# Twelve projection sums in place of sixteen: GpSimd folds four pixels, and the value products come in two pairs

## The reference, cut to what matters

```python
x = features.reshape(b, c, h, s, w, s)                 # s = 4: patches of n = 16 pixels
reduce_feats = x.mean((3, 5))...                       # patch means
unf = ...                                              # (b, hw, n, c)
q = _ln(reduce_feats, ln_q_w, ln_q_b) @ Wq.T
kv = _ln(unf, ln_kv_w, ln_kv_b) @ Wkv.T                # k, v for each of the 16 pixels
attn = softmax(einsum('bhpd,bhpnd->bhpn', q * scale, k), axis=-1)   # over the 16 pixels
aggre = einsum('bhpn,bhpnd->bhpd', attn, v)
return reduce_feats + aggre @ proj_w.T + proj_b
```

## Time and profile before

| | us |
|---|---|
| median of 3 runs | 945.28 (944.91 to 946.49) |
| profiled execution, its time | 945.04 |
| its span, first to last instruction | 943.2 |
| busy in the span: PE / DVE / ACT / POOL | 880.8 / 746.8 / 495.2 / 436.5 |
| mean granted TensorE clock | 0.987 |

### The profile page before, as it was taken

One profiled execution on the slowest core, in us unless ns is written; L12 is line 12 of the kernel. 1 busy time (PEld: TensorE's weight loads), 2 busy tenths in 40 slices (PEclk: granted clock), 3 DMA queues, 4 the chain that ended last, 5 costly groups with the idle time before them and its releaser, 6 DMA issues.

```text
span 943.2 us, 24254 instructions
## 1 busy us (share of the span) xinstructions
PE 880.8 (93%) x9608; PEld 376.9 (40%) x9608; DVE 746.8 (79%) x1271; ACT 495.2 (52%) x767; POOL 436.5 (46%) x259
## 2 busy tenths in 40 slices
PE   5799999999999999999999999859799999999996
PEld 1234334334334334334434434323244444444443
DVE  6688788788788788788788788999577787878775
ACT  3645445445445445445445442437766665666662
POOL 3677677677667667667667661100010110101000
PEclk9999999999999999999999999979799999999999
DMA  9568878878878878878878856100000000000000
GB/s 383 138 189 241 267 208 241 261 212 239 257 219 238 254 225 234 253 230 230 247 240 227 248 154 149 32 0 1 0 1 23 13 12 23 13 23 12 23 12 35
DMA packets 49061, 141.64 MB, mean 150 GB/s; under 512 B 5440, under 2 KB 5440, under 8 KB 40768
## 3 DMA queue, kind: packets, MB, share of 16 engines
q1 hardware_dynamic: 48960, 140.17, 49.9%
HBM read 68.85 MB, written 4.19 MB: 77 GB/s over the span
## 4 chain that ended last, share of the span: by engine, by line
PE 85%; DVE 9%; issue 2%; ACT 2%; DMA 1%; POOL 0%; SPq 0%; DVEq 0%; ACTq 0%; POOLq 0%
PE ring L864 22%; PE bank_ms L836 13%; PE qp L901 12%; PE bank_sq L836 6%; PE ring L1095 5%; DVE sb_prodv L1267 4%; PE ring L1065 4%; PE bank_ms L1107 3%; PE qp L1050 2%; PE bank_sq L1095 2%; PE ring L1010 1%; PE qp L824 1%; PE bank_ms L1065 1%; PE bank_ms L1102 1%; PE ring L1086 1%
## 5 line engine op out<-in xcount | busy, mean ns | idle before, releaser
L864 PE MATMUL ring<-sb_arena,sb_wqkv 64*64 64x512 f32 x2048 | 266.6, 602 | 16.6 <-DVE sb_prodv L1267 15.1
L1267 DVE TENSOR_TENSOR sb_prodv<-ring,sb_wbc 128x1024 f32<-128x1024 f32 x128 | 154.1, 1207 | 33.0 <-PE ring L864 30.1
L1236 DVE TENSOR_TENSOR sb_prodk<-ring,sb_qbuf 128x1024 f32<-128x1024 f32 x128 | 153.3, 1219 | 18.7 <-PE ring L864 15.4
L482 POOL TENSOR_TENSOR sb_rows<-sb_arena 128x2048 f32<-128x2048 f32 x31 | 141.7, 4569 | 15.8 <-DVE sb_sum L474 15.8
L901 PEld LDWEIGHTS qp<-sb_prodv,sb_tok_w 64*64 64x64 f32 x4096 | 119.8, 133 | 52.9 <-issue 49.8
L601 POOL TENSOR_TENSOR sb_parts_q<-sb_arena,sb_const 128x512 fp32r<-128x512 f32 x15 | 15.6, 1039 | 265.8 <-DVE sb_arena L1508 265.8
L901 PE MATMUL qp<-sb_prodv,sb_tok_w 64*64 64x128 f32 x4096 | 128.5, 269 | 1.7 <-DVE sb_prodv L1267 1.7
L645 ACT ACTIVATE sb_xsq<-sb_arena 128x2048 f32<-128x2048 f32 x64 | 118.4, 1896 | 1.3 <-DMA sb_arena<-x 1.3
L864 PEld LDWEIGHTS ring<-sb_arena,sb_wqkv 64*64 64x64 f32 x2048 | 58.4, 132 | 147.9 <-issue 78.8
L566 POOL TENSOR_TENSOR sb_score<-sb_score,sb_smx 128x512 f32<-128x512 f32 x32 | 40.9, 1279 | 79.5 <-DVE sb_smx L1250 79.5
L484 POOL TENSOR_TENSOR sb_rows<-sb_rows 128x1024 f32<-128x1024 f32 x31 | 73.9, 2383 | 2.4
(11 more groups left out here) (243 smaller groups left out, 1439.7 us busy)
## 6 DMA issues: line engine op xcount, KB each, us to landing
sb_arena<-x SPq DMA_DIRECT2D x64, 1024.0 KB, 8.8
sb_wbc<-sb_wgt SPq DMA_DIRECT2D x256, 256.0 KB, 5.7
out<-sb_arena SPq DMA_DIRECT2D x16, 256.0 KB, 2.0
sb_rest_w<-rest_w SPq DMA_DIRECT2D x1, 918.5 KB, 21.4
sb_const<-const SPq DMA_DIRECT2D x1, 264.5 KB, 3.0
sb_tok_w<-tok_w SPq DMA_DIRECT2D x1, 260.5 KB, 2.9
sb_const<-const SPq DMA_DIRECT2D x1, 256.0 KB, 21.6
```

The costliest lines, as they stand in the source:

```text
L482: eng.tensor_tensor(rows[:, :, :, :], pix[:, :, 0:8], pix[:, :, 8:16], ALU.add).then_inc(sum8_ready, 1)
L864: mm = pe.matmul(ring[slot][C * half:C * half + C, i, :], image_block(w, i), x[C * i:C * i + C, m, half, c], start=True, stop=True)
L1236: dve.tensor_tensor(by_pixel(prodk[:, c]), by_pixel(ring[c % 2][:, :, :]), q[:, :, None, :].to_broadcast([P, 2, N_PIX, G32]), ALU.mult).th ...
L1267: dve.tensor_tensor(prodv[:, :, :, G32 * c:G32 * (c + 1)], by_pixel(ring[k % 2][:, :, :]), by_pixel(wbc[:, c]), ALU.mult).then_inc(values_ ...
```

## The change

- GpSimd gets a new operation, `add_pixels(u, k)`. When value product k of unit u is in `prodv`, it adds pixels 12 to 15 of that quarter's 32 patches onto pixels 8 to 11: a [128, 2, 4, 32] float32 addition in place, 256 elements in each partition. There are four in a unit.
- `project` then runs over 12 pixels, in parts 0, 1 and 2. Part 2, which reads pixels 8 to 11, waits for all four additions of its unit (`pixels_added`). Part 3 is gone.
- TensorE's order in a step becomes: keys 0, keys 1, project 0, keys 2, project 1, keys 3, project 2, scores, values 0, values 1, squares, query, values 2, values 3, means.
- GpSimd's order in a step becomes: the first halving of the patch sums of unit n+2, additions 2 and 3 of unit n-1, the other three halvings, the shift of the scores, addition 0 of unit n, the weighing, addition 1, the normalising.
- ScalarE does `query(n+2)` ahead of `pixel_mean(n+2)`. VectorE does `score_sum(n+1)` ahead of `query_var(n+2)`.

```diff
+N_PRE, N_PART = 4, 4
+N_SUM = N_PIX - N_PRE
...
+            def add_pixels(u, k):
+
+                c = VALUE_ORDER[k]
+                pool.wait_ge(values_weighted, NC * u + k + 1)
+                part = prodv[:, :, :, G32 * c:G32 * (c + 1)]
+                pool.tensor_tensor(part[:, :, N_SUM - N_PRE:N_SUM], part[:, :, N_SUM - N_PRE:N_SUM], part[:, :, N_SUM:N_PIX],
+                                   ALU.add).then_inc(pixels_added, 1)
...
             def step(n, m):
-                if not isinstance(n, int) or n + 2 < UNITS:
-                    patch_sums(pool, n + 2, (m + 2) % NF)
-                if not isinstance(n, int) or n + 1 < UNITS:
-                    softmax(n + 1)
+                if nxt2:
+                    patch_sums_first(pool, n + 2, (m + 2) % NF)
+                if prev:
+                    add_pixels(n - 1, 2)
+                    add_pixels(n - 1, 3)
+                if nxt2:
+                    patch_sums_rest(pool, n + 2)
+                if nxt:
+                    shift_scores(n + 1)
+                add_pixels(n, 0)
+                if nxt:
+                    weigh_scores(n + 1)
+                add_pixels(n, 1)
+                if nxt:
+                    norm_scores(n + 1)
             pipeline(pool, step, UNITS)
+            add_pixels(UNITS - 1, 2)
+            add_pixels(UNITS - 1, 3)
...
+                    query(n + 2, m)
                     pixel_mean(n + 2)
-                    query(n + 2, m)
...
-                for n in range(4 * part, 4 * part + 4):
+                if part == N_SUM // N_PART - 1:
+                    pe.wait_ge(pixels_added, NC * u + NC)
+                for n in range(N_PART * part, N_PART * part + N_PART):
...
-                                           prodv[rows_of, i, n, :], start=(n == 0), stop=(n == N_PIX - 1))
-                if part == 3:
+                                           prodv[rows_of, i, n, :], start=(n == 0), stop=(n == N_SUM - 1))
+                if part == N_SUM // N_PART - 1:
                     mm.then_inc(projected_mm, 1)
...
                     project(n - 1, 2)
-                    project(n - 1, 3)
                 if nxt:
                     scores(n + 1)
                 values(n, m, 0)
+                values(n, m, 1)
                 if nxt2:
                     pixel_squares(n + 2, m2)
-                values(n, m, 1)
-                if nxt2:
                     query(n + 2, m2)
...
                 values(n, m, 2)
+                values(n, m, 3)
                 if nxt2:
                     pixel_means(n + 2, m2)
-                values(n, m, 3)
...
+                if nxt:
+                    score_sum(n + 1)
                 if nxt2:
                     query_var(n + 2)
                 if nxt:
-                    score_sum(n + 1)
                     score_inverse(n + 1)
```

More of the change, by code:

```diff
@@ L242, in build @@
         values_weighted = sem("values_weighted")
+        pixels_added = sem("pixels_added")
         projected_mm = sem("projected_mm")
@@ L475, in first_patch_sums, with patch_sums_first @@
                               ALU.add).then_inc(done[3], 1)
-        def patch_sums(eng, u, m):
+        def patch_sums_first(eng, u, m):
             eng.wait_ge(x_in[m], x_count(u, m))
@@ L482, in patch_sums, with patch_sums_rest @@
             eng.tensor_tensor(rows[:, :, :, :], pix[:, :, 0:8], pix[:, :, 8:16], ALU.add).then_inc(sum8_ready, 1)
+        def patch_sums_rest(eng, u):
             eng.wait_ge(sum8_ready, u + 1)
@@ L556, in _, with scores_of, by_patch, shift_scores @@
         def _(pool):
[L557 to L563, removed]
+            def scores_of(a):
+                return a[:, :].rearrange("p (n i) -> p n i", i=G32)
+            def by_patch(a):
+                return a[:, None, :].to_broadcast([P, N_PIX, G32])
+            def shift_scores(u):
                 pool.wait_ge(score_max_ready, u + 1)
-                pool.tensor_tensor(sc, sc, spread(smx), ALU.subtract).then_inc(scores_shifted, 1)
+                pool.tensor_tensor(scores_of(score), scores_of(score), by_patch(smx), ALU.subtract).then_inc(scores_shifted, 1)
+            def weigh_scores(u):
                 pool.wait_ge(scores_exp, u + 1)
@@ L570, in softmax, with norm_scores @@
                 pool.tensor_tensor(wgt[:, :], score[:, :], rstd[:, :], ALU.mult).then_inc(weights_raw, 1)
+            def norm_scores(u):
                 pool.wait_ge(weights_raw, u + 1)
                 pool.wait_ge(inverse_sum_ready, u + 1)
-                pool.tensor_tensor(wg, wg, spread(srz), ALU.mult).then_inc(weights_ready, 1)
-            patch_sums(pool, 1, 1)
-            softmax(0)
-            def step(n, m):
-                if not isinstance(n, int) or n + 2 < UNITS:
-                    patch_sums(pool, n + 2, (m + 2) % NF)
-                if not isinstance(n, int) or n + 1 < UNITS:
-                    softmax(n + 1)
+                pool.tensor_tensor(scores_of(wgt), scores_of(wgt), by_patch(srz), ALU.mult).then_inc(weights_ready, 1)
+            def add_pixels(u, k):
[4 more added lines that the diff above has]
+                                   ALU.add).then_inc(pixels_added, 1)
+            patch_sums_first(pool, 1, 1)
+            patch_sums_rest(pool, 1)
+            shift_scores(0)
+            weigh_scores(0)
+            norm_scores(0)
+            def step(n, m):
+                prev = not isinstance(n, int) or n >= 1
+                nxt = not isinstance(n, int) or n + 1 < UNITS
+                nxt2 = not isinstance(n, int) or n + 2 < UNITS
+                if nxt2:
[13 more added lines that the diff above has]
+                    norm_scores(n + 1)
             pipeline(pool, step, UNITS)
+            add_pixels(UNITS - 1, 2)
+            add_pixels(UNITS - 1, 3)
             pool.wait_ge(rest_in, 16)
@@ L964, in last_step @@
                 values(n, m, 0)
-                for part in range(4):
+                for part in range(N_SUM // N_PART):
                     project(n - 1, part)
```

## The result

The changed kernel takes 922.37 us (median of 4 runs, 920.26 to 924.36) against 945.69 for the kernel before (4 runs). The ratio is 0.9753, 95% interval 0.9722 to 0.9784: 23 us faster, inside the range, 8 us slower than the forecast. The profiled execution took 924.28 us, its span is 922.5.

The account below looks back on a forecast made before the run. TensorE bounds: unit 17.78 us, less 0.71 stall and 0.86 projection part, plus 0.52 scores' wait, gives 16.72; 30 units and 0.2 at the end give 913.3, with 1.2 allowed for ties 914.5 us; range 909 to 926.

Parts of the forecast that it names:

- The signs of being wrong: Wrong if project 2 waits for GpSimd, an addition is above 0.82 us, or keys 2 waits for key product 0.
- A: Rival, GpSimd late: each addition costs 0.95 us instead of 0.74, or as much is lost at waits; 925 us, chance 0.13.
- B: Rival, late keys: mean square and pixel_var delay key product 0 by 0.2 to 0.4 us more; 922 us, chance 0.16.
- The stall before keys 1: On TensorE, keys 1 starts 0.71 us late, waiting for the ring slot of values 3; the new order removes this.
- The projection, and scores waiting for key product 3: On TensorE, one project part fewer saves 0.86 us; scores then stall 0.52 us, starting 2.39 us after keys 3.
- The price of an addition: On GpSimd, 0.74 us per addition, taken from the row L489 of equal size and run length; bounds 0.64 to 1.28.
- GpSimd's loop, 16.47 us with 0.25 of slack: GpSimd's loop through project 2 takes 16.47 us, 0.25 under the 16.72 us unit, so GpSimd does not decide.
- The tie at keys 2: Pixel_var on VectorE precedes key product 0, done 12.52 us after scores; TensorE reaches keys 2 at 12.56; delay lengthens the unit.
- Load of x has whole units of slack. Free.: Among the DMAs, the load of x has whole units of slack and costs nothing.
- The swaps, "costed at nothing": ScalarE's query before mean square and VectorE's sum before query_var fit in waits and cost nothing.
- The end, "net -0.2": Last unit: normalising up to 0.74 us later, projection 0.93 us shorter; net 0.2 us saved.
- the forecast's 31.8 us in the units: Gain over 30 units, each going from 17.78 to 16.72 us.

Follow-up runs that it names:

- e3: Changed kernel with only the new engine orders: 16 pixels projected in four parts, no additions; 926.65 us, unit 17.12 us.
- e4: Changed kernel with only the additions and the 12-pixel projection; value quarters and ScalarE and VectorE orders as before the change; 938.82 us, unit 17.45 us.
- e9: Changed kernel with each GpSimd addition 512 elements in place of 256; 962.25 us, unit 18.22 us.
- e6: Changed kernel with each load of x, from unit 4 on, bringing a quarter of its bytes; 918.38 us, unit 16.80 us.
- e7: Changed kernel with additions 2 and 3 ahead of the first halving on GpSimd; 917.71 us, unit 16.79 us.
- e2: Changed kernel without GpSimd's additions and without TensorE's wait for them, the projection still over 12 pixels; 916.48 us, unit 16.79 us.
- e8: Changed kernel with additions 2 and 3 ahead of the first halving on GpSimd, and values 0 ahead of scores on TensorE; 910.41 us.

## Why the prediction was right, and where its 8 us went

- **The signs of being wrong**: the prediction named three, and two of them came. Project 2 waits for GpSimd (9.6 us in all, in 19 of the steps), and keys 2 waits for key product 0. What makes the gain is right, what limits it is incomplete. The range held the 4.2 us of x only because it had been widened for A and B, and neither of them names x: that part is luck. B has the tie, but at 17.0 us a unit and not 16.79.
- **The stall before keys 1**: right. The rows show keys 0 and 1 on end, and e3 gives 0.66 of the 0.71 us.
- **The projection, and scores waiting for key product 3**: right, 2.38 us against 2.39 from keys 3; e4 comes to 17.45 against 17.43.
- **The price of an addition**: right, 0.734 us. The neighbour of equal size and run length was the row to go by. What the prediction takes from the Trainium skill, "SBUF — State Buffer", section "Who interferes with whom", agrees: VectorE's value products take 1.21 us in the median (1.22 before) with GpSimd busy 91 of 100 us (72 before).
- **GpSimd's loop, 16.47 us with 0.25 of slack**: right in that it does not decide. e9 puts it some 0.2 us shorter.
- **The tie at keys 2**: it lost, as allowed for. Pixel_var waits 0.56 us for ScalarE and holds back key product 0, and keys 2 starts 1.26 to 1.29 us after that in each unit. The unit is 16.78 and not 16.72, 1.8 us in all (1.2 allowed); the jump back every fourth unit adds 0.4.
- **"Load of x has whole units of slack. Free."**: wrong, the step that failed. I had looked for who waits for x and found no wait in the kernel before, and had not counted back from the reader through SyncE's program. The load has to cross eight issues, 6.9 us together, and 9 us of transfer, and the loop over two units closes through the weights. Before the change this left a slack of about 0.8 us and not of whole units; the shorter units used it up. It cost 16.93 - 16.79 = 0.14 us a unit, 4 us in all; e6 and e7 give them back.
- **The swaps, "costed at nothing"**: true of them as made, but the reverse order would have cost 0.35 us a unit. I had found only that they fit, not that they carry.
- **The end, "net -0.2"**: wrong by 5.2 us in the profiled execution. From the last maximum to the start of the last tokens it is 2.1 us longer (22.9 before, 25.0 after). Normalising comes 0.26 us later (0.74 at most was said), and from its end to the value products that wait for its weights it is 7.2 us where it was 5.9. The additions are not the whole cause: e2 has none, its normalising is as early as before, and its stretch is 24.0 us; in e3, with 16 pixels and no additions, it is 25.0. What makes it longer stays open.

  Behind the last tokens the code is the same. It took 343.7 us before and 346.6 here, and 343.5 to 345.0 in the profiles of all ten other kernels. So these 2.9 us belong to this execution and not to the change. 2.5 of them lie in the last 16 us. The same matmuls there, after:

```profile
910.11 1.97 PE L1138 MATMUL bank_ms<-sb_arena,sb_rest_w 128*64 128x512 f32 x4
...
911.86 3.34 PE L1143 MATMUL bank_ms<-sb_arena,sb_rest_w 128*64 128x512 f32 x8
```

  and before:

```profile
932.33 1.08 PE L1102 MATMUL bank_ms<-sb_arena,sb_rest_w 128*64 128x512 f32 x4
933.24 2.12 PE L1107 MATMUL bank_ms<-sb_arena,sb_rest_w 128*64 128x512 f32 x8
```

  The windows of the very end, after and then before; the granted clock is the third number from the end:

```profile
910.00:922.00 12.00, 6.37 (x21) 2.21 (x20) 4.83 (x8) 1.61 (x5) 0.00 (x0) 0.64 0.12 44
...
930.00:943.00 13.00, 6.51 (x34) 3.69 (x32) 5.80 (x9) 2.21 (x6) 0.00 (x0) 0.86 0.11 42
```

  The clock was lower (0.64 against 0.86), and the same work took longer in these rows. A second stretch at a low clock, in the recurrence, is in both kernels alike (0.50 is the lower level, 1.2 GHz). Windows 12 to 22 and 22 to 32 us behind the last tokens, after:

```profile
587.89:597.89 10.00, 4.74 (x12) 1.76 (x10) 10.00 (x44) 0.00 (x0) 0.00 (x0) 0.97 0.00 0
597.89:607.89 10.00, 3.11 (x4) 1.51 (x5) 9.86 (x39) 4.07 (x11) 0.00 (x0) 0.50 0.00 1
```

  and before:

```profile
611.46:621.46 10.00, 5.95 (x14) 2.28 (x12) 10.00 (x45) 0.00 (x0) 0.00 (x0) 1.00 0.00 0
621.46:631.46 10.00, 2.83 (x4) 1.28 (x5) 9.86 (x39) 3.79 (x10) 0.00 (x0) 0.52 0.00 1
```

  Of the changed kernel's four runs two are 4 us shorter (920.3) with a mean clock of 0.985 and 0.989, two (924.3) have 0.981. But two runs of e8 at 0.981 and 0.985 differ by 0.01 us. So the mean clock alone does not explain the 4 us; what does, and what decides when the clock falls, stays open.

Of the forecast's 31.8 us in the units, then, 25.4 came; 2.2 went to the tie and the jump back, and 4.2 to x. These sums are of the profiled execution, which at 924.28 us is 1.9 above the median. That the median lies 8 us above the forecast is therefore partly the luck of which executions were drawn.

## What to carry to other kernels

A transfer that no engine waits for is not thereby free: the load of x had about 0.8 us of slack. Count from its issue back to what lets it be issued, and forward to its reader; where the two lie in one loop with the engine that gets more work, the slack shrinks with each microsecond saved. And a queue is a place in line for bytes as well as for instructions: here, moving 2 MB up moved four small transfers back, and cost 137 us.

When a unit's length differs from one unit to the next, the shortest units show what the schedule allows (16.78), and the long ones point, by their waits, at what varies. Units that are long at a fixed distance, here every fourth, point at the program's own loop.

## What the runs showed of the hardware

- DMAs of 256 KB, the last four of them issued behind 2 MB in SyncE's queue, took up to 12.4 us to land (7.0 otherwise), and the unit was 21.5 us long; behind 0.5 MB it was up to 6.9 us and 16.87.
- Eight such DMAs took SyncE 6.4 to 7.4 us to issue.
- The price of a GpSimd addition went by its elements: 0.734 us for 256 in place in `prodv` (0.735 for the fourth halving's 256), 1.28 for 512 (e9's additions in place, and the third halving), with VectorE working beside it.
- In the recurrence of both kernels TensorE was busy 4.7 to 6.0 of 10 us at a clock of 0.97 to 1.00, and then 2.8 to 3.1 of 10 us at 0.50 to 0.52. At the very end of the changed kernel's profiled execution the clock was 0.64 where it was 0.86 before, and four matmul records of 512 columns took 1.97 us in place of 1.08.
- Jumping back to the start of a four-unit loop body made VectorE's next instruction start 0.06 to 0.1 us later; on a tie that went into the unit one for one.
